# Dense graph attention on one core: three rotating PSUM banks, rows of the next block made early, and every second Relu of head 1 on VectorE

## The chip, the core and the metric

The kernel runs on one core of a Trainium2 chip. A core has TensorE (PE, matmuls into PSUM), VectorE (DVE), ScalarE (ACT), GpSimd (POOL) and SyncE, which each work through a queue of their own, and 16 DMA engines. The metric is the device time of one execution in microseconds; the profile is one execution recorded by the hardware profiler.

## The reference

Four residual layers act on a graph of 3125 nodes with 128 features and 100000 edges, each after a layer norm and a Relu: a mean over neighbours, three layers of graph attention, an aggregation with minimum, maximum and deviation, and a two-layer mean. The change is in the second of them. Its core, cut:

```python
xs = (h @ Ws).reshape(N, H, C)                  # H = 4 heads of C = 32
alpha_s, alpha_d = sum(xs * a_s), sum(xd * a_d)
e = leaky_relu(alpha_s[src] + alpha_d[dst], 0.2)
ex = exp(e - segment_max(e, dst)[dst])
alpha = ex / (segment_sum(ex, dst)[dst] + EPS)
out = segment_sum(xs[src] * alpha[:, :, None], dst) + bias
# three times, with a relu between
```

## The kernel before

Attention is computed densely. A matrix A of edge counts (source by target) was made earlier; for each pair of nodes the weight is the count times the exponential. A layer `g` goes over 8 blocks `J` of 400 targets (`CH`), a block over 25 tiles `n` of 128 sources (`NT`), so a layer has 200 tiles and the stage 600. In a tile each of the four heads passes through a "soft" buffer of 128x400:

- Heads 0 and 1: ScalarE makes a Relu of the block's row plus the source's number (`half_bend`, L879), two tiles ahead; GpSimd adds another row to both heads in one instruction of 128x800 (L719). Together these are the leaky Relu.
- Heads 2 and 3: VectorE makes it in one instruction (`bend`, L1853), from a row that stays in PSUM (`psV`) and one in SBUF.
- ScalarE takes the exponential of each head into PSUM (`exponent`, L891). There are three banks for it: `psE[2]` and `psE[3]` are the same one.
- VectorE caps it and multiplies by the counts, back into the soft buffer (`weigh`, L1861).
- TensorE sums over the sources (L1302) with an operand `xs_1` in which the features of a head stand beside 32 columns of ones: 64 columns give numerator and denominator of a head. Heads 0 and 1 go into `psL`, heads 2 and 3 into `psZ`, each pair as two column tiles.

At a block's end ScalarE copies the denominators (`totals`, L869), VectorE divides (`divide`, L1885 and L1888), ScalarE writes the new features (`layer_rows`, L861). TensorE opens the accumulators of the next block (L1298) when `divide` has read them.

Each block needs rows of its own, made in tiles 16 to 23 of the block before: `levels` is 25 matmuls into `psR` (L1230), VectorE's `highest` takes the top level out of the exponent's bits (L1829, L1830), `top_rows` and `own_rows` are two matmuls with four output rows (L1236, L1240), VectorE's `top` and `near` work on four partitions (L1835, L1841 to L1843), `spread_row` spreads each of four rows over 128 partitions (L1247), ScalarE's `near_row` copies it out (L854, L856), `keep_rows` writes the two rows that stay in PSUM (L1253). The order of the work on each engine is written out by hand in the loops over `t`; between engines stand only semaphores. `summed` counts the tiles that TensorE has summed: the soft buffers have four places for heads 0 and 1 (`A_SLOTS`) and three for heads 2 and 3 (`MOVING`).

Of the kernel before, what the change touches and what calls it, by code (L numbers as in the profile page):

```python
# [5 lines left out]
ALU = mybir.AluOpType  # L6
# [8 lines left out]
H = 4  # L15
# [59 lines left out]
def build(nc, x, src, dst, W0, b0, Ws, Wd, att_s, att_d, gat_b, M_w, M_b, U_w, U_b, gamma, beta,  # L75
# [42 lines left out]
    with ExitStack() as ctx:  # L118
# [31 lines left out]
        LEV = XSW + NT * 6 * C  # L150
        ROWV = LEV + NT * H * LEVELS // 2
        SOFT = MB
        LAST_ROW = SOFT + MOVING * 2 * CH
        BIGW = max(ROOT + NT * D, MB + 2 * DENSE_T * W, LAST_ROW + CH)
        assert ROWV + 9 * CH <= U
# [63 lines left out]
        psE = [quad[:, 512 * i:512 * i + CH] for i in (0, 1, 2, 2)]  # L219
# [66 lines left out]
        for t in range(STEPS):  # L286
# [21 lines left out]
        xs_1 = words(XSW, NT * 6 * C).rearrange("p (t a k) -> p t a k", t=NT, a=2)  # L308
# [6 lines left out]
        row_2 = [words(ROWV, 2 * CH), words(ROWV + 6 * CH, 2 * CH)]  # L315
        row_8 = [[words(ROWV + 4 * CH, CH), words(ROWV + 5 * CH, CH)], [words(ROWV + 8 * CH, CH), words(LAST_ROW, CH)]]
        row_2v = [[words(ROWV + 2 * CH, CH), words(ROWV + 3 * CH, CH)],
                  [apart[:, 3 * NT * H + P // 2 + CH // 2 + h * CH:3 * NT * H + P // 2 + CH // 2 + (h + 1) * CH] for h in range(2)]]
        level = apart[:, 2 * LANE - LEVELS:2 * LANE]
        assert 3 * NT * H + P // 2 + CH // 2 + 2 * CH <= 2 * LANE - LEVELS - 7 * H  # L320
# [3 lines left out]
        bits = lane_x[:].rearrange("p a w -> p (a w)")[:, 0:CH]  # L324
        m_4 = bits[0:H, :]
        v_4 = Z[0:H, 0:CH]
        share = sm[:, 0:CH]
        to_all = lane_s[0:H, :, :]
# [3 lines left out]
        def soft(n, h):  # L332
            if h < 2:
                return pick[:, (2 * (n % A_SLOTS) + h) * CH:(2 * (n % A_SLOTS) + h + 1) * CH]
            return words(SOFT + (2 * (n % MOVING) + h - 2) * CH, CH)

# [102 lines left out]
        sel_rdy = sem("sel_rdy")  # L439
        xs_ps, xs_rdy = sem("xs_ps"), sem("xs_rdy")  # L440
        reach_rdy, reach_ps, diag_rdy = sem("reach_rdy"), sem("reach_ps"), sem("diag_rdy")
# [3 lines left out]
        half_a, bent_p, bent_v, near_ps, soft_rdy = sem("half_a"), sem("bent_p"), sem("bent_v"), sem("near_ps"), sem("soft_rdy")  # L445
# [212 lines left out]
        def _(pool):  # L658
# [55 lines left out]
            for n in range(NT * NH):  # L714
# [3 lines left out]
                pool.wait_ge(half_a, 2 * n + 2)  # L718
# [37 lines left out]
        def _(act):  # L756
# [92 lines left out]

            def near_row(J, h):  # L850

                act.wait_ge(row_ps, H * J + h + 1)
                if h < 2:
                    nc.scalar.mul(row_8[J % 2][h], psR, 1.0 - NEG_SLOPE)  # L854
                to = row_2[J % 2][:, CH * h:CH * h + CH] if h < 2 else row_2v[J % 2][h - 2]
                nc.scalar.mul(to, psR, NEG_SLOPE).then_inc(row_rdy, 1)  # L856

            def layer_rows(g, J):

                act.wait_ge(share_rdy, 4 * (J + 1))  # L860
# [20 lines left out]
            def exponent(n, h):  # L881

                if h == 0:
                    act.wait_ge(bent_p, n + 1)
                elif h >= 2:
                    act.wait_ge(bent_v, 2 * n + h - 1)
                if h < 3 and n:
                    act.wait_ge(weight_rdy, H * n + (-3, -2, 0)[h])
                if h == 3:
                    act.wait_ge(weight_rdy, H * n + 3)  # L890
                nc.scalar.activation(psE[h], soft(n, h), ACT.Exp, bias=s_all[:, 2, n % NT, h:h + 1]).then_inc(soft_rdy, 1)  # L891
# [3 lines left out]
            for g in range(3):  # L895
                for t in range(NT):
# [3 lines left out]
                    for k in range(2):  # L900
                        ins = nc.scalar.copy(xs_1[:, t, :, 2 * C * k:2 * C * k + C],
                                             psY[t % 2][:, 0:D].rearrange("p (a h c) -> p h a c", a=2, h=2)[:, k, :, :])
                    ins.then_inc(xs_rdy, 1)
                act.wait_ge(lev_rdy, 2 * g + 1)
                nc.scalar.activation(lev, lev, ACT.Exp, scale=STEEP * 0.6931471805599453).then_inc(xs_rdy, 1)
                for c in range(NCH):
                    J = NCH * g + c
                    if c == 0:
                        for h in range(H):
                            near_row(J, h)  # L910
                        for n in range(NT * J, NT * J + 2):
                            half_bend(n, 0)
                            half_bend(n, 1)
                    for t in range(NT):
                        n = NT * J + t
                        ahead = c < NCH - 1 or t < NT - 2
# [12 lines left out]
                        if c < NCH - 1 and 19 <= t < 19 + H:  # L929
                            near_row(J + 1, t - 19)  # L930
# [155 lines left out]
        def _(pe):  # L1086
# [134 lines left out]
            def levels(g, J):  # L1221

                for late in range(2):
                    k = 2 * J + late
                    pe.wait_ge(a_part[k % RING], 16 * (k // RING + 2))
                pe.wait_ge(lev_rdy, 2 * g + 2)
                if J:
                    pe.wait_ge(row_rdy, H * J)
                for t in range(NT):
# [857 lines left out]
```

## Time and profile before

| | us |
|---|---|
| median of three runs | 5264.95 (5263.87 to 5265.28) |
| the profiled execution | 5259.3, span 5257.5 |
| busy in the span: TensorE / VectorE / ScalarE / GpSimd | 3943.7 / 3670.2 / 3263.5 / 1873.8 |
| GpSimd's adds of the attention (L719), 600 | 1131.4 |
| exponentials (L891), 2400 | 705.8 + 659.1 |
| weightings (L1861), 2400 | 682.4 + 650.0 |

The profiled execution's time is 1.8 us more than its span, which lies between its first and its last instruction. Busy time counts an engine's own instructions; an engine that is idle may be waiting for another, and the timeline names in brackets for how long and for whom.

### The profile page before, as it was taken

Reading aid. Unit: us, or ns where it says so; the run is one execution under the profiler, and the core shown is the slowest. Engines: PE = TensorE matmul, PEld = TensorE weight load, DVE = VectorE, ACT = ScalarE, POOL = GpSimd, SP = SyncE. Lnnn points to the kernel's source line nnn. Section 1 sums busy time; section 2 is a strip of 40 time slices with the busy share of each in tenths; the row PEclk is TensorE's granted clock in tenths of the full one; section 3 lists DMA queues with packets and bytes.
Section 4 is the critical chain, followed back from the end, with each engine's and each line's share of the span. In section 5 each row is a group of like instructions: output and inputs, shape, how many; then the busy total and the mean of one; then the engine's idle time right before and its main releaser. Section 6 shows DMA issues by size and latency. Waiting matters only on the chain.

```text
span 5257.5 us, 59119 instructions
## 1 busy us (share of the span) xinstructions
PE 3943.7 (75%) x16302; PEld 1689.8 (32%) x16302; DVE 3670.2 (70%) x8162; ACT 3263.5 (62%) x7606; POOL 1873.8 (36%) x1368
## 2 busy tenths in 40 slices
PE   6999796666666666666666666666669999986899
PEld 3444344111111121111112111111137667654444
DVE  8999784777777757777775777777767777774311
ACT  5888404777667756777775777777757667674100
POOL 0000131444333323333332434444437777773000
PEclk9999896676766666666666676766679999997899
DMA  4444642111111101111111111111026776763566
GB/s 154 157 154 155 228 167 72 39 39 58 39 39 39 60 19 40 39 39 60 40 39 39 40 39 39 39 39 58 0 85 231 239 240 232 241 217 105 183 229 224
DMA packets 387474, 552.25 MB, mean 105 GB/s; under 512 B 23781, under 2 KB 358021, under 8 KB 386922
## 3 DMA queue, kind: packets, MB, share of 16 engines
q1 hardware_dynamic: 358114, 494.48, 27.1%
q0 software_dynamic: 23024, 48.93, 3.4%
q10 hardware_dynamic: 6040, 5.35, 0.4%
q8 instruction: 130, 2.13, 0.2%
q14 instruction: 166, 1.36, 0.1%
HBM read 352.81 MB, written 195.86 MB: 104 GB/s over the span
## 4 chain that ended last, share of the span: by engine, by line
DVE 34%; ACT 19%; PE 17%; issue 11%; DMA 6%; POOL 3%; SPq 2%; ACTq 0%; DVEq 0%; POOLq 0%
DVE pick L1861 12%; PE quad L1109 7%; ACT quad L891 7%; DVE big L1861 6%; ACT pick L879 6%; DVE big L1853 6%; DMA src_bc<-pe_src_d 3%; POOL big L736 2%; PE psS L1230 2%; DMA big<-table_d,src_win 2%; DVE big L1982 2%; PE psZ L1302 2%; PE quad L1430 1%; DVE sm L1885 1%; ACT hT L977 1%
## 5 line engine op out<-in xcount | busy, mean ns | idle before, releaser
L719 POOL TENSOR_TENSOR pick<-pick,big 128x800 f32<-128x800 f32 x600 | 1131.4, 1886 | 1913.7 <-ACT pick L879 1913.7
L891 ACT ACTIVATE quad<-big,keep 128x400 f32<-128x400 f32 x1200 | 705.8, 588 | 770.1 <-DVE big L1861 770.1
L1302 PE MATMUL psZ<-big 128*64 128x400 f32 x2400 | 799.3, 758 | 469.6 <-DVE big L1861 468.2
L1302 PE MATMUL psL<-pick,big 128*64 128x400 f32 x2400 | 794.5, 754 | 207.2 <-DVE pick L1861 206.4
L1861 DVE SCALAR_TENSOR_TENSOR pick<-quad,big 128x400 f32<-128x400 f32 x1200 | 650.0, 572 | 303.3 <-ACT quad L891 302.7
L1861 DVE SCALAR_TENSOR_TENSOR big<-quad,big 128x400 f32<-128x400 f32 x1200 | 682.4, 569 | 113.1 <-ACT quad L891 113.1
L736 POOL DMA_INDIRECT big<-table_d,src_win x672 | 645.4, 960 | 279.5 <-issue 189.3
L879 ACT ACTIVATE pick<-big,keep 128x400 f32<-128x400 f32 x1200 | 735.0, 613 | 0.5
L891 ACT ACTIVATE quad<-pick,keep 128x400 f32<-128x400 f32 x1200 | 659.1, 579 | 3.1 <-POOL pick L719 3.1
L1302 PEld LDWEIGHTS psZ<-big 128*64 128x64 f32 x2400 | 161.2, 179 | 1066.9 <-DVE big L1861 1042.2
L1982 DVE SCALAR_TENSOR_TENSOR big<-big,keep_win,quad 128x256 f32<-128x256 f32 x784 | 375.8, 479 | 152.0 <-ACT quad L1010 81.6
L1302 PEld LDWEIGHTS psL<-pick,big 128*64 128x64 f32 x2400 | 161.2, 178 | 778.0 <-DVE pick L1861 712.4
L795 ACT COPY big<-quad 128x512 f32<-128x512 f32 (+1 forms) x21 | 11.3, 540 | 466.2 <-PE quad L1109 466.2
L1109 PE MATMUL quad<-big 128*128 128x512 f32 (+1 forms) x700 | 278.5, 559 | 6.2 <-issue 5.6
L1376 PE MATMUL psH<-big,pick 128*128 128x384 bf16 x700 | 233.6, 335 | 57.8 <-DVE big L1971 49.6
L831 ACT ACTIVATE big<-quad 128x400 bf16<-128x400 f32 x496 | 232.2, 503 | 57.5 <-PE quad L1169 50.4
L1009 ACT COPY quad<-big 128x128 f32<-128x128 f32 x784 | 199.7, 255 | 108.1 <-DMA big<-table_d,src_win 67.4
L708 POOL TENSOR_TENSOR keep<-big 128x512 f32<-128x512 f32 (+1 forms) x7 | 8.1, 1152 | 685.0 <-DMA big<-A_d 605.2
L1376 PE MATMUL psH<-big,hT 128*128 128x384 bf16 x700 | 232.1, 332 | 22.1 <-DVE big L1971 21.5
L1376 PE MATMUL psS<-big,pick 128*128 128x384 bf16 x700 | 233.3, 334 | 0.0
L1376 PE MATMUL psS<-big,hT 128*128 128x384 bf16 x700 | 231.7, 332 | 0.0
L1010 ACT ACTIVATE quad<-big 128x128 f32<-128x128 f32 x784 | 212.9, 272 | 0.0
(361 smaller groups left out, 6474.5 us busy)
## 6 DMA issues: line engine op xcount, KB each, us to landing
big<-A_d SPq DMA_DIRECT2D x17, 6400.0 KB
rows_d<-big SPq DMA_DIRECT2D x112, 896.0 KB
A_d<-big SPq DMA_DIRECT2D x396, 200.0 KB, 1.9
big<-A_d SPq DMA_DIRECT2D x24, 2600.0 KB, 9.9
big<-A_d SPq DMA_DIRECT2D x24, 2400.0 KB, 9.4
big<-A_d SPq DMA_DIRECT2D x32, 1600.0 KB, 11.0
big<-table_d,src_win POOLq DMA_INDIRECT x672
src_bc<-pe_src_d SPq DMA_DIRECT2D x56, 64.0 KB
```

Source lines behind the costliest of these rows:

```text
L719: pool.tensor_tensor(soft_2[n % A_SLOTS], soft_2[n % A_SLOTS], row_2[J % 2], ALU.add).then_inc(bent_p, 1)
L736: pool.indirect_dma_start(out=rows[:, k, 0:p.table_w], out_offset=None, in_=table_d, in_offset=bass.IndirectOffsetOnAxis(ap=src_win[:, s, ...
L831: nc.scalar.activation(hot_q[:, t % HOTS, j, :], psD[(dist0[t] + n) % 4][:, 0:QW], ACT.Relu).then_inc(hot_s, 1)
L879: nc.scalar.activation(soft(n, h), row_8[J % 2][h], ACT.Relu, bias=s_all[:, 1, t, h:h + 1]).then_inc(half_a, 1)
L891: nc.scalar.activation(psE[h], soft(n, h), ACT.Exp, bias=s_all[:, 2, n % NT, h:h + 1]).then_inc(soft_rdy, 1)
L1010: nc.scalar.mul(psA[n % len(psA)][:, D:2 * D], rows[:, k, :], -1.0).then_inc(sq_rdy, 1)
L1109: ins = nc.tensor.matmul(psT[at % 2][:, 0:n * W].rearrange("f (b w) -> f b w", w=W), rows[:, s, :], abuf[(at + 1) % 2][:, 0:n, W * s:W * s ...
L1302: ins = nc.tensor.matmul(acc[a][64 * k:64 * k + 64, 0:CH], xs_1[:, t, a, C * k:C * k + 2 * C], soft(n, 2 * a + k), start=False, stop=(t == ...
L1376: ins = nc.tensor.matmul(psP[i][:, 0:3 * D].rearrange("p (c w) -> p c w", c=3), is_src[q % 2][:, t, i * P:(i + 1) * P], table_s[:, t, :, 0 ...
L1853: v.scalar_tensor_tensor(soft(n, 2 + h), psV[h], s_all[:, 1, t, 2 + h:3 + h], row_2v[J % 2][h], ALU.add, ALU.max).then_inc(bent_v, 1)
L1861: v.scalar_tensor_tensor(soft(n, h).rearrange("p (b w) -> p b w", w=W), psE[h].rearrange("p (b w) -> p b w", w=W), CAP, a, ALU.min, ALU.mu ...
L1982: v.scalar_tensor_tensor(state[:, k, :], prev[k], kw[:, 1, k:k + 1], psA[n % len(psA)][:, 0:2 * D], ALU.min, ALU.max).then_inc(updated, 1)
```

## The change

Of the four parts, one is on VectorE's and ScalarE's tile: the exponentials go through three banks in turn (`psW`), in the order of heads 3, 0, 1, 2, and an exponential waits for the weighting that was three places earlier. VectorE's `bend` of head 2 is made in the tile itself, that of head 3 one tile ahead. The second: for odd tiles the Relu of head 1 is made on VectorE (`half_bend(n)`, one `tensor_scalar`), and GpSimd's add then waits for both makers. The third: numerators and denominators have banks of their own, `acc[0]` (`psL`) and `acc[1]` (`psZ`), in eight matmuls of 32 columns behind the last weighting of a tile; ScalarE copies both banks (`totals`) and VectorE divides in SBUF. The fourth: the rows of the next block are begun in tile 1, `levels` is given out over tiles 3 to 17, the near rows are cut into three bf16 parts (`cut_row`, `middle_part`) that lie in partitions 0, 32 and 64, and are spread by matmuls in bf16. The scale of the rows is changed by the factor 0.2 of the leaky Relu.

```diff
-        psE = [quad[:, 512 * i:512 * i + CH] for i in (0, 1, 2, 2)]
+        psW = [quad[:, 512 * i:512 * i + CH] for i in range(3)]
...
+        BANK_ORDER = (3, 0, 1, 2)
+        EXP_AT = (2, 3, 4, 1)
+        WEIGH_AT = (2, 3, 4, 1)
+
+        def bank(n, h):
+            return psW[(H * n + BANK_ORDER.index(h)) % len(psW)]
+
+        def bank_free(n, h):
+            at = H * n + BANK_ORDER.index(h) - len(psW)
+            return H * (at // H) + WEIGH_AT[BANK_ORDER[at % H]] if at >= 0 else 0
...
-                pool.wait_ge(half_a, 2 * n + 2)
+                pool.wait_ge(half_a, halves(n))
+                if n % 2:
+                    pool.wait_ge(half_v, n // 2 + 1)
...
             def totals(J):
                 act.wait_ge(summed, NT * (J + 1))
-                for h in range(H):
-                    total = (C, 2 * C)[h % 2]
-                    ins = nc.scalar.copy(share[C * h:C * h + C, :], acc[h // 2][total:total + C, 0:CH])
-                ins.then_inc(totals_rdy, 1)
+                if J:
+                    act.wait_ge(share_rdy, J)
+                nc.scalar.copy(share, acc[0][:, 0:CH])
+                nc.scalar.copy(total_b, acc[1][:, 0:CH]).then_inc(totals_rdy, 1)
...
             def exponent(n, h):
-                if h == 0:
-                    act.wait_ge(bent_p, n + 1)
-                elif h >= 2:
-                    act.wait_ge(bent_v, 2 * n + h - 1)
-                if h < 3 and n:
-                    act.wait_ge(weight_rdy, H * n + (-3, -2, 0)[h])
-                if h == 3:
-                    act.wait_ge(weight_rdy, H * n + 3)
-                nc.scalar.activation(psE[h], soft(n, h), ACT.Exp, ...)
+                act.wait_ge((bent_p, bent_p, bent_2, bent_3)[h], n + 1)
+                if bank_free(n, h):
+                    act.wait_ge(weight_rdy, bank_free(n, h))
+                nc.scalar.activation(bank(n, h), soft(n, h), ACT.Exp, ...)
...
                     for t in range(NT):
-                        exponent(n, 0)
-                        exponent(n, 1)
-                        exponent(n, 2)
-                        if ahead:
-                            half_bend(n + 2, 0)
-                        exponent(n, 3)
-                        if ahead:
-                            half_bend(n + 2, 1)
-                        if c and t == 0:
+                        exponent(n, 3)
+                        if left > 2:
+                            half_bend(n + 2, 0)
+                        exponent(n, 0)
+                        if left > 1 and n % 2:
+                            half_bend(n + 1, 1)
+                        exponent(n, 1)
+                        exponent(n, 2)
+                        if c and t == 1:
                             totals(J - 1)
-                        if c and t == 2:
+                        if c and t == 6:
                             layer_rows(g, J - 1)
-                        if c < NCH - 1 and 19 <= t < 19 + H:
-                            near_row(J + 1, t - 19)
+                        if c < NCH - 1:
+                            if t == 3:
+                                own_row(J + 1)
+                            if t == 20:
+                                middle_part(J + 1)
+                            if t == 21 or t == 22:
+                                near_row(J + 1, t - 21)
+                            if t == 23:
+                                near_row(J + 1, 2)
+                                near_row(J + 1, 3)
...
+            def weighted_sums(n):
+                J, t = n // NT, n % NT
+                if t == 0:
+                    if J:
+                        pe.wait_ge(totals_rdy, J)
+                    nc.tensor.matmul(acc[1][:, 0:CH], of_eps[0:1, :], ones_row[0:1, :], start=True, stop=False)
+                pe.wait_ge(weight_rdy, H * n + H)
+                for h in range(H):
+                    nc.tensor.matmul(acc[0][C * h:C * h + C, 0:CH], xs_1[:, t, C * h:C * h + C], soft(n, h), ...)
+                for h in range(H):
+                    ins = nc.tensor.matmul(acc[1][C * h:C * h + C, 0:CH], ones[:, 0:C], soft(n, h), ...)
+                ins.then_inc(summed, 1)
...
                         if c < NCH - 1:
-                            if t == 16:
-                                levels(g, J + 1)
...
+                            if t == 1:
+                                own_rows(g, J + 1)
+                            if 3 <= t < 16:
+                                levels(g, J + 1, t - 3, t - 2)
+                            if t == 16 or t == 17:
+                                levels(g, J + 1, SPLIT + 6 * (t - 16), SPLIT + 6 * (t - 15))
+                            if t == 18:
+                                top_rows(J + 1)
+                            if 20 <= t < 23:
+                                spread_row(J + 1, t - 20)
+                            if t == 23:
+                                spread_row(J + 1, 3)
+                                keep_row(J + 1, 1)
+                                keep_row(J + 1, 0)
...
+            def cut_row(J):
+                high = parts[J % 2][0:H, :]
+                link(v.tensor_copy(high, v_4))
+                link(v.tensor_tensor(m_4, v_4, high, ALU.subtract))
+                link(v.tensor_copy(mid_4, m_4))
+                v.tensor_tensor(parts[J % 2][64:64 + H, :], m_4, mid_4, ALU.subtract).then_inc(near_rdy, 1)
...
+            def half_bend(n):
+                if n >= A_SLOTS:
+                    dve.wait_ge(summed, n - A_SLOTS + 1)
+                v.tensor_scalar(soft(n, 1), row_8[J % 2][1], s_all[:, 1, t, 1:2], 0.0, ALU.add, ALU.max).then_inc(half_v, 1)
...
+            def divide(J):
+                dve.wait_ge(totals_rdy, J + 1)
+                link(v.reciprocal(total_b, total_b))
+                v.tensor_tensor(share, share, total_b, ALU.mult).then_inc(share_rdy, 1)
...
             def tile_weights(n, left):
-                weigh(n, 0)
-                weigh(n, 1)
-                if bends:
-                    bend(n + 1, 0)
-                weigh(n, 2)
-                if bends:
-                    bend(n + 1, 1)
-                weigh(n, 3)
+                weigh(n, 3)
+                bend(n, 0)
+                weigh(n, 0)
+                if left > 1 and n % 2 == 0:
+                    half_bend(n + 1)
+                if left > 1:
+                    bend(n + 1, 1)
+                weigh(n, 1)
+                weigh(n, 2)
...
                         tile_weights(n, NT * (NCH - c) - t)
+                        if c and t == 3:
+                            divide(J - 1)
                         if c < NCH - 1:
-                            if t == 16:
+                            if t == 18:
                                 highest(J + 1)
-                            if t == 17:
-                                top(J + 1)
-                            if t == 18:
+                            if t == 19:
                                 near(J + 1)
-                        if c and t == 0:
-                            divide(J - 1)
+                                cut_row(J + 1)
```

The rows below are the instructions in the order in which each engine gets them, with the semaphores that they wait for. VectorE, one tile in mid-block before (`pick` is a soft buffer of head 0 or 1, `big` one of head 2 or 3):

```order
L1861 SCALAR_TENSOR_TENSOR pick<-quad,big 128x400 [waits soft_rdy] x2
L1853 SCALAR_TENSOR_TENSOR big<-quad,keep,big 128x400 [waits summed]
L1861 SCALAR_TENSOR_TENSOR big<-quad,big 128x400 [waits soft_rdy]
L1853 SCALAR_TENSOR_TENSOR big<-psH,keep,big 128x400 [waits summed]
L1861 SCALAR_TENSOR_TENSOR big<-quad,big 128x400 [waits soft_rdy]
```

VectorE, the same place now, an even tile (the first row is head 2 of the tile before and head 3 of this one):

```order
L1918 SCALAR_TENSOR_TENSOR big<-quad,big 128x400 [waits soft_rdy] x2
L1901 SCALAR_TENSOR_TENSOR big<-quad,keep,big 128x400 [waits summed]
L1918 SCALAR_TENSOR_TENSOR pick<-quad,big 128x400 [waits soft_rdy]
L1911 TENSOR_SCALAR pick<-big,keep 128x400 [waits summed]
L1901 SCALAR_TENSOR_TENSOR big<-psH,keep,big 128x400 [waits summed]
```

The weighting of head 3 has moved to the front, and the Relu (L1911) stands behind the weighting of head 0.

TensorE, the last matmuls of a block and the first of the next, before:

```order
L1302 MATMUL psZ<-big 64x400 [waits weight_rdy]
L1302 MATMUL psZ<-big 64x400
L1298 MATMUL psL<-keep 128x400 [waits share_rdy]
L1302 MATMUL psL<-pick,big 64x400 [waits weight_rdy]
L1302 MATMUL psL<-pick,big 64x400
L1298 MATMUL psZ<-keep 128x400 [waits share_rdy]
```

and now (the tile's last denominators, the opening, and the next tile's sums):

```order
L1303 MATMUL psZ<-big,ones 32x400 x2
L1297 MATMUL psZ<-keep 128x400 [waits totals_rdy]
L1300 MATMUL psL<-pick,big 32x400 [waits weight_rdy]
L1300 MATMUL psL<-pick,big 32x400
L1300 MATMUL psL<-big 32x400 x2
L1303 MATMUL psZ<-pick,ones 32x400 x2
```

One opening is left, it waits for ScalarE's copies instead of VectorE's division, and all sums of a tile stand behind one wait.

ScalarE, tiles 23 and 24 of a block now (L888 copies rows 2 and 3 of the next block):

```order
L918 ACTIVATE quad<-big,keep 128x400 [waits weight_rdy,bent_2]
L888 COPY big<-psS 128x400 [waits row_ps] x2
L918 ACTIVATE quad<-big,keep 128x400 [waits weight_rdy,bent_3]
L911 ACTIVATE pick<-big,keep 128x400 [waits summed]
L918 ACTIVATE quad<-pick,keep 128x400 [waits weight_rdy,bent_p] x2
```

Both copies stand in one tile, ahead of the exponentials of the last one; before, the four rows were copied in four tiles, 19 to 22.

## Rows read from the trace of the kernel before

**Rows 1.** Busy time of each engine in the first attention layer (stretch, length, engines, clock).

```profile
core 0: us, PE busy (x) PEld busy (x) DVE busy (x) ACT busy (x) POOL busy (x), PEclk, DMA share, GB/s
890.00:1844.00 954.00, 639.14 (x1950) 152.43 (x1948) 704.00 (x1282) 684.63 (x1301) 377.09 (x200) 0.69 0.14 43
```

**Rows 2.** Timeline, tiles in mid-block (start, duration, engine, line; idle time in brackets).

```profile
1190.40 1.09 DVE L1861 SCALAR_TENSOR_TENSOR pick<-quad,big 128x400 f32<-128x400 f32 x2 [0.46 <-ACT quad L891]
...
1191.41 0.63 DVE L1853 SCALAR_TENSOR_TENSOR big<-quad,keep,big 128x400 f32<-128x400 f32 x1
...
1191.95 0.56 DVE L1861 SCALAR_TENSOR_TENSOR big<-quad,big 128x400 f32<-128x400 f32 x1
...
1192.43 0.62 DVE L1853 SCALAR_TENSOR_TENSOR big<-psH,keep,big 128x400 f32<-128x400 f32 x1
...
1192.61 0.60 ACT L891 ACTIVATE quad<-big,keep 128x400 f32<-128x400 f32 x1 [0.65 <-DVE big L1861]
...
1193.14 0.61 ACT L879 ACTIVATE pick<-big,keep 128x400 f32<-128x400 f32 x1
...
1193.24 0.57 DVE L1861 SCALAR_TENSOR_TENSOR big<-quad,big 128x400 f32<-128x400 f32 x1 [0.18 <-ACT quad L891]
...
1193.66 1.10 ACT L891 ACTIVATE quad<-pick,keep 128x400 f32<-128x400 f32 x2
...
1193.83 1.89 POOL L719 TENSOR_TENSOR pick<-pick,big 128x800 f32<-128x800 f32 x1 [1.99 <-ACT pick L879]
...
1194.27 1.09 DVE L1861 SCALAR_TENSOR_TENSOR pick<-quad,big 128x400 f32<-128x400 f32 x2 [0.46 <-ACT quad L891]
```

**Rows 3.** Timeline, GpSimd's add of the same tile in two successive blocks.

```profile
1139.05 1.88 POOL L719 TENSOR_TENSOR pick<-pick,big 128x800 f32<-128x800 f32 x1 [8.87 <-ACT pick L879]
...
1258.71 1.89 POOL L719 TENSOR_TENSOR pick<-pick,big 128x800 f32<-128x800 f32 x1 [8.57 <-ACT pick L879]
```

**Rows 4.** Timeline, operations at a change of block.

```profile
1198.57 4.59 PE L1230 MATMUL psS<-big 128*128 128x400 bf16 x25
...
1203.19 0.57 DVE L1829 TENSOR_SCALAR lane_x<-psS 128x400 int32<-128x400 int32 x1 [5.51 <-PE psS L1230]
...
1203.80 0.37 DVE L1830 TENSOR_SCALAR lane_x<-lane_x 128x400 f32<-128x400 int32 x1
...
1210.57 0.68 DVE L1835 TENSOR_SCALAR lane_x<-psS,ends 4x400 f32<-4x400 f32 x1 [3.12 <-PE psS L1236]
...
1217.66 0.56 DVE L1841 TENSOR_TENSOR Z<-lane_x,psS 4x400 f32<-4x400 f32 x1 [3.12 <-PE psS L1240]
...
1218.25 0.35 DVE L1842 TENSOR_SCALAR Z<-Z 4x400 f32<-4x400 f32 x1
...
1249.21 0.98 ACT L869 COPY sm<-psZ 32x400 f32<-32x400 f32 x2
...
1250.22 2.65 DVE L1885 RECIPROCAL sm<-sm 128x400 f32<-128x400 f32 x1 [1.97 <-ACT sm L869]
...
1254.13 0.51 PE L1298 MATMUL psL<-keep 1*128 1x400 bf16 x1 [8.59 <-DVE sm L1888]
```

**Rows 5.** Timeline, VectorE's L1719 beside GpSimd's additions and without them.

```profile
688.21 8.85 POOL L711 TENSOR_TENSOR keep<-keep,big 128x512 f32<-128x512 f32 x6
...
693.15 1.23 DVE L1719 TENSOR_SCALAR has<-deg 128x4 f32<-128x4 f32 x1
...
783.73 0.16 DVE L1719 TENSOR_SCALAR has<-deg 128x4 f32<-128x4 f32 x1
```

**Rows 6.** Timeline, TensorE: one matmul alone, and pairs of column tiles.

```profile
1238.75 0.93 PE L1253 MATMUL quad<-Z,lane_s 4*128 4x400 f32 x2 [0.66 <-DVE big L1853]
...
1240.63 0.89 PE L1302 MATMUL psL<-pick,big 128*64 128x400 f32 x4
...
2028.64 1.60 PE L1302 MATMUL psZ<-big 128*64 128x400 f32 x4 [0.96 <-DVE big L1861]
...
2030.19 1.60 PE L1302 MATMUL psL<-pick,big 128*64 128x400 f32 x4
```

More of the change, by code:

```diff
@@ L847, in _, with own_row, middle_part @@
             normalize(1)
+            def own_row(J):
+                act.wait_ge(lev_ps, 3 * J + 1)
+                nc.scalar.mul(own_4, psR[0:H, :], NEG_SLOPE).then_inc(lead_rdy, 1)
+            def middle_part(J):
+                act.wait_ge(near_rdy, 2 * J + 2)
+                nc.scalar.copy(parts[J % 2][32:32 + H, :], mid_4).then_inc(lead_rdy, 1)
             def near_row(J, h):
@@ L899, in _ @@
                     act.wait_ge(xs_ps, NT * g + t + 1)
[L900 to L903, printed above, removed]
+                    nc.scalar.copy(xs_1[:, t, :], psY[t % 2][:, 0:D]).then_inc(xs_rdy, 1)
                 act.wait_ge(lev_rdy, 2 * g + 1)
@@ L1218, in _, with own_rows @@
             pe.wait_ge(node_out, NT)
[L1221 to L1226, printed above, removed]
+            def own_rows(g, J):
                 if J:
                     pe.wait_ge(row_rdy, H * J)
-                for t in range(NT):
+                nc.tensor.matmul(psR[0:H, :], w_att[:, g, D + H:D + 2 * H], feat[g % 2][:, CH * (J % NCH):CH * (J % NCH + 1)],
+                                 start=True, stop=True).then_inc(lev_ps, 1)
@@ L1230, in levels @@
+            def levels(g, J, first, last):
+                if first == 0:
+                    pe.wait_ge(lead_rdy, 2 * J + 1)
+                for t in range(first, last):
+                    if t == 0 or t == SPLIT:
+                        k = 2 * J + (t == SPLIT)
+                        pe.wait_ge(a_part[k % RING], 16 * (k // RING + 2))
                     ins = nc.tensor.matmul(psR.rearrange("l (b w) -> l b w", w=W), lev[:, t, :, :].rearrange("p h k -> p (h k)"),
                                            marks_of(J, t), start=(t == 0), stop=(t == NT - 1))
-                ins.then_inc(lev_ps, 1)
+                if last == NT:
+                    ins.then_inc(lev_ps, 1)
@@ L1243, in spread_row @@
             def spread_row(J, h):
-                pe.wait_ge(near_rdy, 3 * J + 3)
                 if h:
                     pe.wait_ge(row_rdy, H * J + h)
-                nc.tensor.matmul(psR, to_all[:, h, :], v_4, start=True, stop=True).then_inc(row_ps, 1)
-            def keep_rows(J):
-                for h in range(2):
-                    if J:
-                        pe.wait_ge(bent_v, 2 * NT * J - 1 + h)
-                    nc.tensor.matmul(psV[h], to_all[:, 2 + h, :], v_4, start=True, stop=True).then_inc(near_ps, 1)
@@ L1288, in _ @@
+                        keep_row(J, 0)
                     for t in range(NT):
                         n = NT * J + t
[L1290 to L1303 removed]
@@ L1880, in tile_weights @@
                     dve.sem_inc(ring_used, 1)
-            def divide(J):
-                dve.wait_ge(totals_rdy, J + 1)
-                link(v.reciprocal(share, share))
-                for h in range(H):
-                    own = (0, 3 * C)[h % 2]
-                    v.tensor_tensor(share[C * h:C * h + C, :], acc[h // 2][own:own + C, 0:CH], share[C * h:C * h + C, :],
-                                    ALU.mult).then_inc(share_rdy, 1)
             for g in range(3):
@@ L1896, in _ @@
                         highest(J)
-                        top(J)
                         near(J)
-                        bend(NT * J, 0)
+                        cut_row(J)
                         bend(NT * J, 1)
```

153 lines of the change are left out of this document (74 added, 79 removed).

## The prediction

> **What bounds the kernel now.** I read first the busy times by stage. The three attention layers take more than half of the span, and in the first of them no engine is full: in 954 us VectorE is busy 704, ScalarE 685, TensorE 639 and GpSimd 377 us, for 200 tiles [rows 1]. So this stage is set by waits in a ring, not by one engine's work. The timeline of one tile in mid-block shows the ring [rows 2]. Heads 2 and 3 share a PSUM bank (`psE`), so the exponential of head 3 starts only when VectorE has weighted head 2 (1192.61, 0.65 us idle in front of it, released by L1861). From there: exponential, then Relu (0.53 from start to start), exponential of head 0 (0.52), and 0.61 until VectorE weighs it (1194.27); on VectorE two weightings (1190.40 to 1191.41, 1.01), a bend (0.54), the weighting of head 2 (0.56) and 0.10 until ScalarE starts. These make 3.87, and the weightings of head 0 are indeed 3.87 apart (1190.40, 1194.27). A tile has six ScalarE instructions 0.52 apart (3.1) and on VectorE four weightings (0.48 apart) and two bends (0.54), 3.0: both engines idle some 0.8 us in each tile because of that bank.
>
> The second cost is the change of block. GpSimd's adds of like place in two successive blocks are 119.66 apart [rows 3]; 25 tiles explain 96.8, so 22.8 us go at each change, in the serial passage through level sums, rows and totals. Per layer: 200 tiles x 3.87 = 774, 7 changes x 22.8 = 160, and 20 for the ends, together 954.
>
> **The change, part by part.** *The tile.* Three banks rotate over the heads, so an exponential waits only for the weighting three places earlier: that ring is gone. VectorE gets 300 Relus (every second one of head 1), ScalarE loses them. No row shows such a Relu; the nearest is the two-operation pass over 128x400 in SBUF, 0.37 us (1203.80) [rows 4]; the bounds are 0.28 and 0.63 (a bend). By work alone a tile then costs VectorE 3.02 + 0.19 = 3.2 and ScalarE 5.5 x 0.52 = 2.9.
>
> What sets the tile is, I think, another ring, which the new Relu closes. It stands on VectorE behind the weighting of head 0 of an even tile n, and GpSimd's add for tile n+1 waits for it; the exponential of head 0 of n+1 waits for the add; ScalarE's Relu for n+2 stands behind that exponential; the add for n+2 waits for this Relu, and the weighting of head 0 of n+2, behind it the next VectorE Relu, for that add. Priced from [rows 2, 4]: Relu 0.37, step to GpSimd 0.08 (1193.14 + 0.61 to 1193.83), add 1.89, step to ScalarE 0.10 (the only such step shown is VectorE's, 1191.95 + 0.56 to 1192.61), exponential to the next ScalarE instruction 0.52, Relu 0.61, step 0.08, add 1.89, step 0.10, exponential 0.58, step 0.03, weighting 0.48. Sum 6.73 for two tiles, 3.37 for one. It exceeds the 3.2 of VectorE, so it decides, by little. Now the add is hidden wholly: ScalarE makes both Relus of a tile two tiles ahead, so the add is done long before its exponential. In the new order that cover is gone.
>
> *TensorE.* Per tile it had four sums with 64 output columns in two pairs; it gets eight with 32 columns, four into `psL`, four into `psZ`, all behind the last weighting. Two side by side cost as much as one: four records in 0.89 at the high clock (1240.63), one matmul's two in 0.93 (1238.75), and at the low clock pairs follow each other 1.55 apart [rows 6]. If four also go side by side a tile costs 2 x 1.55 = 3.1 at 1.2 GHz and about 1.7 at 2.4 GHz. Then the sums of tile n must end before ScalarE's first Relu of n+4, about 3.1 us behind the last weighting of n: just enough even at the low clock. The Trainium skill (TensorE: Matmul & The Clock Gate, "Part 3: Packing small matmuls") measures 2.38 times for three column tiles. By that efficiency, as an estimate from the page, four would take 1.26 times one, some 3.9 us a tile at the low clock and 2.0 at the high; no row here shows four.
>
> *The change of block.* Five items, each against the end E of the tile's last weighting, when ScalarE has been free for 0.66 us. (a) The sums of a block's tile 0 now wait until ScalarE has copied both totals at the end of tile 1: 2 x 0.5 (1249.21), 0.06, the opening matmul 0.44 (1254.13), then 3.1, so E + 4.0. ScalarE needs that for a Relu that it reaches at E + 0.9, and the copies themselves cost it 1.0: with 0.2 slack, 4.0. The other inserted work (a row on ScalarE, the level sums, 0.18 each by 1198.57, one per tile from tile 3) lies beside the tiles: 1.0, bounds 0 and 3. (b) The division: 2.65 (1250.22) and one product of 0.57, 3.25; I add 0.95 for the port, below: 4.2. (c) Bits of the top level: 0.61 + 0.28 (1203.19, 1203.80), and half a microsecond until the last six level sums are done: 1.4. (d) Near rows and their cut into three bf16 parts: eight linked passes on four partitions, 0.68, then 0.56 and 0.36 in turn (1210.57, 1217.66, 1218.25), 4.25 with the gaps, and 0.95 for the port: 5.2. (e) Copies of the four rows: the first two hold ScalarE 1.0 each, of which 0.3 is slack, and the first also waits some 0.5. The fourth is queued directly behind the third in tile 23, but its matmul stands behind that tile's sums: ScalarE stops until E + 3.8 (low clock) or E + 2.2, and all exponentials of tile 24 queue behind it; 4.1 between the two. Together 6.0. Sum 21.8, with bounds 16 and 28: hardly less than the 22.8 of now. Many waits were taken out, but three new ones (a, d, e) stand in single queues.
>
> *The port.* The trace shows that a VectorE pass from SBUF to SBUF can be held while GpSimd adds: 128x4 elements took 1.23 us beside an add (693.15) and 0.16 without (783.73) [rows 5]. The Trainium skill (SBUF — State Buffer, "SBUF: two separate sides") calls it an exclusive lock, held for the whole instruction; the trace agrees. For the new Relu it should cost nothing: the weighting ahead of it needs the add of tile n, and the add of n+1 needs the Relu, so no add is in flight. The passes of (b) and (d) can meet one: 0 to 1.89, depending on whether the tile's number is odd, on average 0.95 each.
>
> *The rest.* The passage at the head of a layer trades shorter bf16 spreads for the longer cut; the copies of the features before it hide behind TensorE's matmuls. I take both at nothing, bounds 10 us faster or slower in all.
>
> **Sum.** Per layer 200 x 3.37 = 673, 7 x 21.8 = 153, ends 20: 846 instead of 954, 108 less, 325 for three. The profiled execution took 5259.3 (span 5257.5), so 4934; the runs' median is 5.65 higher: **4940 us**.
>
> **The rivals.**
> - *VectorE bounds and the changes of block are hidden better* (the high clock holds, no port waits): T = 3.2, b = 16 give 772 a layer, 4725. For it: the ring exceeds VectorE's work by only 0.17. Against: rows (d) and (e) are serial whatever the clock. Chance 0.12.
> - *TensorE becomes the bound*: of four column tiles only two run together. Four rounds of 0.78 at the high clock, which such a busy engine would keep, 3.1, with levels and mode changes about 3.6; everything that waits for it at a block's change is later, b = 28: 720 + 196 + 20 = 936, 5210. Against: two tiles show no loss. Chance 0.15, a quarter of it no longer faster. The 2.38 of the Trainium skill's page named above would put TensorE between this case and the forecast.
> - *Slower: the eight sums run one after another.* 8 x 0.78 = 6.2 a tile at the high clock, 200 x 6.2 + 7 x 16 + 20 = 1372 a layer, 6520. It decides from 4.2 us of TensorE a tile on (954 less 7 x 16, by 200). For it: no 32-column matmul is in the trace. Against: pairs do overlap. Chance 0.05.
> - *Slower: each VectorE Relu meets an add after all*, up to 1.89, of which the ring passes on most: 300 x 1.7 = 510, 5450. By the order of the waits it cannot. Chance 0.03.
> - *The new waits eat all the gain*: b = 38 by (a) and (e) at the low clock throughout: 5270. Chance 0.05.
>
> **How the numbers follow.** The forecast itself has 0.60 and its own range of 4800 to 5060 (T 3.3 to 3.45, b 18 to 26). Below it lies the first rival, above it the second. Leaving out the lowest of the one, and the last three rivals with part of the second, the range is 4760 to 5120. A run of this kernel can tell 0.2% (10 us) from no change. Faster: 0.60 + 0.12 + 0.11 of the second rival + 0.01 of the last = 0.84; same 0.03 (0.01 and 0.02 of the same two); slower 0.13, the rest.
>
> **What would show it.** In mid-block GpSimd's adds stand in pairs, 6.7 us for two, each released by VectorE's Relu and ScalarE's in turn; VectorE idles before the weighting of head 0, released by ScalarE, which waits for GpSimd; hardly any wait of head 3 for head 2. The new Relu takes 0.3 to 0.45. Eight matmuls fill 3.1 (low clock) or 1.7. At a block's change: ScalarE idle 3 to 4 us before the Relu in tile 2, and 2 to 4 before the fourth row copy. Wrong it would be if VectorE is full in mid-block (tile at 3.2), if the eight matmuls take over 4 us, if the Relu's mean is over 1 us, or if a change of block costs less than 16 or more than 28.

## The result, and the profile after

The changed kernel takes **4827.6 us** (4824.3 to 4836.7) against 5264.4 of the kernel before: a ratio of 0.917 (95% interval 0.916 to 0.919), 437 us faster where 325 were forecast. The profiled execution has a span of 4828.8 instead of 5257.5, 428.7 less.

The busy times of the first layer, from its first add to its last (columns as in [rows 1], whose stretch was a little wider):

```profile
880.00:1675.00 795.00, 435.89 (x3420) 115.12 (x3420) 715.99 (x1377) 621.96 (x1171) 376.34 (x200) 0.86 0.15 49
```

VectorE is now busy 90% of the layer. In mid-block (the middle tiles of a block of 25) GpSimd's adds follow one another in unequal steps (timeline of GpSimd: start, duration, and in brackets its idle time and who ended it):

```profile
920.73 1.89 POOL L741 TENSOR_TENSOR pick<-pick,big 128x800 f32<-128x800 f32 x1 [1.26 <-ACT pick L911]
924.33 1.88 POOL L741 TENSOR_TENSOR pick<-pick,big 128x800 f32<-128x800 f32 x1 [1.72 <-DVE pick L1911]
927.48 1.89 POOL L741 TENSOR_TENSOR pick<-pick,big 128x800 f32<-128x800 f32 x1 [1.26 <-ACT pick L911]
```

One release by ScalarE's Relu, one by VectorE's, and 6.75 us for the two: 3.375 a tile. The links of that ring, from one VectorE Relu to the next, stand in the timeline of all engines:

```profile
1034.61 0.42 DVE L1911 TENSOR_SCALAR pick<-big,keep 128x400 f32<-128x400 f32 x1
...
1035.17 1.88 POOL L741 TENSOR_TENSOR pick<-pick,big 128x800 f32<-128x800 f32 x1 [1.72 <-DVE pick L1911]
...
1037.09 0.60 ACT L918 ACTIVATE quad<-pick,keep 128x400 f32<-128x400 f32 x1 [0.34 <-POOL pick L741]
1037.62 0.61 ACT L911 ACTIVATE pick<-big,keep 128x400 f32<-128x400 f32 x1
...
1038.31 1.88 POOL L741 TENSOR_TENSOR pick<-pick,big 128x800 f32<-128x800 f32 x1 [1.26 <-ACT pick L911]
...
1040.23 1.12 ACT L918 ACTIVATE quad<-pick,keep 128x400 f32<-128x400 f32 x2
...
1040.86 0.58 DVE L1918 SCALAR_TENSOR_TENSOR pick<-quad,big 128x400 f32<-128x400 f32 x1
...
1041.35 0.42 DVE L1911 TENSOR_SCALAR pick<-big,keep 128x400 f32<-128x400 f32 x1
```

The Relu ends at 1035.03, the add starts 0.14 later; it ends at 1037.05, the exponential of head 0 starts 0.04 later; ScalarE's next Relu ends at 1038.23, and the next add starts 0.08 later. It ends at 1040.19, the next exponential of head 0 starts 0.04 later, VectorE's weighting follows, and behind it the next Relu at 1041.35. From Relu to Relu VectorE is busy 6.58 of 6.75 us, so by its busy share alone it would seem to be the bound; experiment 1 tells the two apart. Among ScalarE's waits in the layers none of an exponential for a weighting is left.

TensorE at its two clocks (two tiles; each matmul leaves two records, which stand in successive rounds, and x2 counts the records of two heads):

```profile
1036.58 0.53 PE L1300 MATMUL psL<-pick,big 128*32 128x400 f32 x2 [1.59 <-DVE big L1918]
1036.60 0.53 PE L1300 MATMUL psL<-big 128*32 128x400 f32 x2
...
1036.94 0.51 PE L1300 MATMUL psL<-pick,big 128*32 128x400 f32 x2
...
1037.62 0.51 PE L1303 MATMUL psZ<-pick,ones 128*32 128x400 f32 x2
...
1059.73 0.88 PE L1300 MATMUL psL<-pick,big 128*32 128x400 f32 x2 [7.29 <-DVE big L1918]
...
1061.73 0.88 PE L1303 MATMUL psZ<-pick,ones 128*32 128x400 f32 x2
```

The granted clock is 1.00 from 1036 to 1039.5 and 0.50 from 1059.5 to 1062. Four rounds start 0.67 apart at the low level (1.2 GHz) and 0.35 at the high one (2.4 GHz), 2.7 and 1.4 us a tile: the records of all four heads start within 0.02 us of each other, so all four column tiles run side by side.

At a change of block, from the timeline of the second block:

```profile
1052.61 2.13 POOL L741 TENSOR_TENSOR pick<-pick,big 128x800 f32<-128x800 f32 x1 [1.26 <-ACT pick L911]
1053.04 1.92 DVE L1888 CAST big<-Z 4x400 bf16<-4x400 f32 x1
...
1061.66 1.89 POOL L741 TENSOR_TENSOR pick<-pick,big 128x800 f32<-128x800 f32 x1 [6.92 <-DVE pick L1911]
...
1074.10 0.49 ACT L888 COPY big<-psS 128x400 f32<-128x400 f32 x1 [3.37 <-PE psS L1283]
```

The cast of a near row takes 1.92 us beside an add (in every second block; 0.36 in the blocks between), and ScalarE stops 3.37 before the copy of the fourth row. The waits of ScalarE between 890 and 3400 us, nearly the whole of the three layers (total, times, longest), show both stops that the prediction placed in ScalarE's queue:

```profile
ACT quad L918 <- DVE big L1901: 284.6, 313, 4.7
ACT quad L918 <- POOL pick L741: 89.9, 261, 1.0
ACT big L888 <- PE psS L1283: 64.5, 37, 4.1
ACT pick L911 <- PE psZ L1303: 61.4, 21, 3.0
```

L888 copies the rows (item e), L911 is the Relu that waits for the sums held back by the totals (item a), 21 times for 21 changes.

**Where the 429 us came from.** From the start of the first add to that of the last the three layers take 794.7, 797.6 and 797.7 (before 928.7, 934.6, 928.7): 402 less. The first add of all starts 10.6 earlier, the two gaps between layers are 6.0 shorter each, the time after the last add 4.0.

### The profile page after: what moved, and what is told of

Read it like the earlier page. It is cut to its first block, busy times and chain, and to the rows that moved or that the text cites. A ratio compares the mean times of both kernels' runs of the same rounds, so it can differ in the third digit from the quotient of the medians.

```text
span 4828.8 us, 69161 instructions
## 1 busy us (share of the span) xinstructions
PE 3370.3 (70%) x20934; PEld 1591.1 (33%) x20934; DVE 3734.0 (77%) x8487; ACT 3100.6 (64%) x7231; POOL 1875.8 (39%) x1368
## 4 chain that ended last, share of the span: by engine, by line
DVE 36%; PE 17%; POOL 11%; ACT 10%; issue 7%; DMA 7%; SPq 2%; POOLq 0%; DVEq 0%; ACTq 0%
DVE pick L1918 9%; POOL pick L741 8%; DVE big L1901 7%; DVE big L1918 7%; PE quad L1143 7%; ACT quad L918 4%; POOL big L758 3%; DMA big<-table_d,src_win 3%; DMA src_bc<-pe_src_d 3%; DVE pick L1911 2%; PE psL L1300 2%; DVE big L2035 2%; PE psZ L1303 2%; PE quad L1475 1%; DVE lane_x L1924 1%
## 5 line engine op out<-in xcount | busy, mean ns | idle before, releaser
L1300 PE MATMUL psL<-pick,big 128*32 128x400 f32 x2400 | 629.8, 609 | 946.7 <-DVE big L1918 945.8
L1918 DVE SCALAR_TENSOR_TENSOR pick<-quad,big 128x400 f32<-128x400 f32 x1200 | 682.7, 569 | 100.9 <-ACT quad L918 100.6
L1300 PE MATMUL psL<-big 128*32 128x400 f32 x2400 | 629.9, 609 | 0.0
L1303 PE MATMUL psZ<-pick,ones 128*32 128x400 f32 x2400 | 609.4, 592 | 0.0
L1303 PE MATMUL psZ<-big,ones 128*32 128x400 f32 x2400 | 609.3, 591 | 0.0
L911 ACT ACTIVATE pick<-big,keep 128x400 f32<-128x400 f32 x900 | 552.7, 615 | 61.9 <-PE psZ L1303 61.4
L1300 PEld LDWEIGHTS psL<-pick,big 128*32 128x32 f32 x2400 | 97.7, 118 | 1218.1 <-DVE big L1918 1191.7
L1901 DVE SCALAR_TENSOR_TENSOR big<-psH,keep,big 128x400 f32<-128x400 f32 x600 | 375.5, 626 | 17.3 <-ACT big L888 17.3
L1901 DVE SCALAR_TENSOR_TENSOR big<-quad,keep,big 128x400 f32<-128x400 f32 x600 | 374.2, 624 | 0.0
L1303 PEld LDWEIGHTS psZ<-pick,ones 128*32 128x32 f32 x2400 | 161.3, 128 | 332.2 <-issue 332.2
```

The costliest lines, as they stand in the source:

```text
L911: nc.scalar.activation(soft(n, h), row_8[J % 2][h], ACT.Relu, bias=s_all[:, 1, t, h:h + 1]).then_inc(half_a, 1)
L1300: nc.tensor.matmul(acc[0][C * h:C * h + C, 0:CH], xs_1[:, t, C * h:C * h + C], soft(n, h), start=(t == 0), stop=(t == NT - 1))
L1303: ins = nc.tensor.matmul(acc[1][C * h:C * h + C, 0:CH], ones[:, 0:C], soft(n, h), start=False, stop=(t == NT - 1))
L1901: v.scalar_tensor_tensor(soft(n, 2 + h), psV[h], s_all[:, 1, t, 2 + h:3 + h], row_2v[J % 2][h], ALU.add, ALU.max).then_inc((bent_2, bent_3 ...
L1918: v.scalar_tensor_tensor(soft(n, h).rearrange("p (b w) -> p b w", w=W), bank(n, h).rearrange("p (b w) -> p b w", w=W), CAP, a, ALU.min, AL ...
```

## Experiments

All are edits of the changed kernel; times are medians, compared with its 4827.6. Beside the experiments the kernel before took 5258.6 to 5264.4, so a few us between two kernels tell nothing. "Layers" is the sum of the three stretches from first to last add, 2390.0 there.

**1. The Relus back on ScalarE.**

```diff
-                        if left > 1 and n % 2:
-                            half_bend(n + 1, 1)
+                        if left > 2:
+                            half_bend(n + 2, 1)
...
-                if left > 1 and n % 2 == 0:
-                    half_bend(n + 1)
```

(with the counts that GpSimd waits for, and the first Relus of a layer)

> All Relus of head 1 go back to ScalarE, both Relus of a tile made two tiles ahead; the rest as in the change. Ring theory (the add's release by VectorE's late Relu sets 3.375 us a tile): that ring is gone, a tile costs ScalarE's six instructions, 3.12 to 3.2, so 600 x 0.2 = 120 us faster than the change: 4710 (4660 to 4770); GpSimd's adds stand evenly, none released by VectorE. Rival (balance: the new kernel gains because ScalarE was relieved): ScalarE at 3.2 plus its waits is the bound, 3.45 to 3.6 a tile, 4870 to 4960.

4740.2 us, ratio to before 0.901 (0.899 to 0.902); layers 2291.3. The adds stand evenly:

```profile
1030.66 1.88 POOL L739 TENSOR_TENSOR pick<-pick,big 128x800 f32<-128x800 f32 x1 [1.23 <-ACT pick L909]
1033.77 1.88 POOL L739 TENSOR_TENSOR pick<-pick,big 128x800 f32<-128x800 f32 x1 [1.24 <-ACT pick L909]
```

3.11 apart, against 3.375. The Relu takes 0.33 us of VectorE's time (1034.61 to 1034.94, where the `bend` behind it starts), 0.17 a tile; a VectorE that was simply full would have given back that much, and the tile gave back 0.26. So the part of the change that moves Relus to VectorE costs 87 us: the gain comes from the other parts, and the ring through VectorE's Relu limits them. The balance theory falls. Now ScalarE sets the tile: from 1114 to 1135 it is busy for all of the 21.00 us. With it full, a change of block costs more, 20.5 instead of 17.9 us, which takes 55 of the 155 us that 600 tiles gave. The edit alters two things, the engine of the Relu and how far ahead it is made (two tiles instead of one); all Relus on ScalarE one tile ahead were not tried.

**2. VectorE's Relu one tile earlier.**

```diff
-                if left > 1 and n % 2 == 0:
-                    half_bend(n + 1)
+                if left > 2 and n % 2:
+                    half_bend(n + 2)
```

(with the first such Relu ahead of each layer's tiles)

> VectorE keeps its 300 Relus but makes each two tiles ahead of its tile instead of one. Ring theory: the ring opens, a tile costs VectorE's work, 3.2, 600 x 0.17 = 100 us faster than the change: 4725 (4690 to 4780), Relu still 0.42. Lock theory (the Relu may stand only where no add is in flight): the Relu now meets GpSimd adds, its mean goes to 0.9 to 1.6, VectorE's tile to 3.45 to 3.8, 4870 to 5080.

4984.5 us, ratio 0.947 (0.946 to 0.948), 157 slower than the change. The lock theory held. Groups of VectorE and GpSimd, and one of the Relus beside its add:

```profile
L1911 DVE TENSOR_SCALAR pick<-big,keep 128x400 f32<-128x400 f32 x300 | 370.6, 1235 | 0.0
...
1246.82 1.87 POOL L741 TENSOR_TENSOR pick<-pick,big 128x800 f32<-128x800 f32 x1 [2.52 <-ACT pick L911]
1246.90 2.01 DVE L1911 TENSOR_SCALAR pick<-big,keep 128x400 f32<-128x400 f32 x1
```

In the change the same 300 Relus take 125.5 us, 418 ns each. The hold adds 245 us of VectorE's time; less the 100 that the open ring was expected to be worth, 145 slower would follow, as an estimate; 157 were measured. In this place the Relu is early and meets the adds; other early places were not tried.

**3. Heads 2 and 3 share a bank again, heads 0 and 1 have their own.**

```diff
-            return psW[(H * n + BANK_ORDER.index(h)) % len(psW)]
+            return psW[min(h, 2)]
```

(with the waits for a free bank that belong to it)

> The rotation is undone alone: heads 0 and 1 have a bank each and heads 2 and 3 share one, as before the change; the rest as in the change. Theory (the shared bank made the old ring): the ring from the weighting of head 2 to the exponential of head 3 is back, with the new Relu in it every second tile, 3.9 to 4.1 us a tile, 600 x 0.5 to 0.7 = 315 to 430 us slower than the change: 5140 to 5260. Rival (the gain comes from the new sums, the Relu and the passage, not from the banks): a tile stays at 3.4 to 3.5, 4830 to 4900.

5116.5 us, ratio 0.972 (0.970 to 0.973), 289 slower, a little less than the range expected. ScalarE's largest wait is again the exponential of head 3 for the weighting of head 2 (L1917; the row is of 890 to 3400 us, and the third layer ends at 3692):

```profile
ACT quad L917 <- DVE big L1917: 506.1, 459, 1.8
```

In the change that wait does not occur. Eight tiles from the middle of a block cost 4.04 each (median of the 24 blocks; the change has 3.39 by that measure). Without the rotation two thirds of the gain are gone.

**4. The fourth row's spread ahead of the sums of tile 23.**

```diff
+                        if c < NCH - 1 and t == 23:
+                            spread_row(J + 1, 3)
                         weighted_sums(n)
...
                             if t == 23:
-                                spread_row(J + 1, 3)
```

> The spread of the fourth row stands on TensorE ahead of the sums of tile 23 instead of behind them. Theory of item (e): ScalarE's stop of 3.3 us before the fourth copy shrinks to 0.7, a block's change costs 1.3 to 2.6 us less, 21 changes: 27 to 55 us faster than the change, 4785 (4770 to 4805). Rival (the time is lost anyway to the next wait, that for the totals in tile 1): within 10 us of 4828.

4794.6 us, ratio 0.911 (0.910 to 0.912), 33 faster; layers 2351.6. Of the same waits:

```profile
ACT pick L911 <- PE psZ L1303: 61.6, 21, 3.0
...
ACT big L888 <- PE psS L1283: 18.5, 35, 0.7
```

The stop for the fourth row is down to 18.5 us in all, the other is untouched. ScalarE waits 46 us less, and the layers are 38 shorter.

**5. The totals copied at the end of tile 0** (`if c and t == 0:` instead of `t == 1`).

> ScalarE copies the totals of the block before at the end of tile 0 instead of tile 1. Theory of item (a): the sums of tile 0 are no longer late by the copies, ScalarE's 3 us before the Relu of tile 2 go, 21 x 2 to 3 = 42 to 63 us faster than the change, 4775 (4760 to 4800). Rival (the copies then wait for the last sums of the block before, so the stop only moves): within 15 us of 4828, or up to 20 us slower.

4791.7 us, ratio 0.910 (0.908 to 0.911), 36 faster, short of the 42 expected; layers 2343.5, 46 less. The Relu's wait of 61.4 is gone; the copies themselves (L901) now wait a little for the last sums of the block before:

```profile
ACT big L888 <- PE psS L1283: 67.8, 30, 4.2
...
ACT sm L901 <- PE psZ L1303: 17.8, 21, 2.3
```

**6. Both moves.**

> The two moves together: the fourth row's spread ahead of the sums of tile 23, the totals at the end of tile 0. Theory (items (a) and (e) are stops in different tiles, each paid by itself): the gains add, 33 + 36 us, 4759 (4750 to 4770). Rival (they share one delay, so that the second finds little left): 35 to 45 us, 4785 to 4793.

4732.0 us, ratio 0.900 (0.899 to 0.901): 96 faster, more than the sum of 69; layers 2292.6, 97 less against 38 and 46. That lies outside the ranges of both theories. The moves do not share a delay; together they gain somewhat more than apart, and why was not settled. The waits of rows and totals on ScalarE fell together from 64.5 + 61.4 + 4.6 to 22.7 + 0 + 7.6, 100 us.

**7. Both moves, and all Relus on ScalarE.**

> All Relus on ScalarE, and the two moves. Theory (the tile costs ScalarE's 3.18 and the stops at a block's change go besides): 4740 - 69 = 4671 (4655 to 4690). Rival (ScalarE, now full, has no slack in which the copies of rows and totals could lie, so the moves bring half): 4705 (4690 to 4740).

**4636.4 us**, ratio 0.882 (0.880 to 0.883): 191 faster than the change, and below the theory's range. The theory took the moves at 69 us together; beside experiment 1 they gave 104, near the 96 of experiment 6. In mid-block ScalarE is full (21.00 of 21 us, 1104 to 1125), but over 400 us with changes of block in them it is busy 356, VectorE 376: the slack lies at the changes, and there the moves still paid. This is the best of the kernels run.

**8. The division behind an odd tile.**

```diff
-                        if c and t == 3:
+                        if c and n % 2 and t in (3, 4):
                             divide(J - 1)
```

> The division of a block's sums stands behind tile 3 or 4, whichever has an odd number in the whole count, instead of always behind tile 3. Theory of the port (behind an even tile GpSimd's add for the tile after next starts while VectorE is in the division and holds its product, 1.49 instead of 0.57 us; behind an odd tile no add can start): the product takes 0.57 in all blocks, 11 blocks x 0.9 = 10 us faster than the change, 4818 (4810 to 4828). Rival (the longer product is hidden in the ring or has another cause): products of 1.49 remain, within 5 us of 4828.

4831.8 us, ratio 0.919 (0.917 to 0.920): no gain. The product's three durations (shortest, median, longest in ns), first in the change, then here:

```profile
L1925 DVE TENSOR_TENSOR sm<-sm,lane_x x24: 574/1030/1487, 994.2 to 3411.2; 128x400 f32<-128x400 f32 x24
```

```profile
L1925 DVE TENSOR_TENSOR sm<-sm,lane_x x24: 574/574/575, 1006.1 to 3419.3; 128x400 f32<-128x400 f32 x24
```

Half the theory: the hold comes by the tile's parity, as said, and goes with it; but the time did not follow. The adds around a division with a held product in the change, then the same adds here, and ScalarE's wait for the fourth row here (64.5, 37, 4.1 in the change):

```profile
993.41 1.87 POOL L741 TENSOR_TENSOR pick<-pick,big 128x800 f32<-128x800 f32 x1 [1.26 <-ACT pick L911]
1000.71 1.89 POOL L741 TENSOR_TENSOR pick<-pick,big 128x800 f32<-128x800 f32 x1 [5.42 <-DVE pick L1911]
```

```profile
1001.98 1.89 POOL L741 TENSOR_TENSOR pick<-pick,big 128x800 f32<-128x800 f32 x1 [1.26 <-ACT pick L911]
1008.67 1.89 POOL L741 TENSOR_TENSOR pick<-pick,big 128x800 f32<-128x800 f32 x1 [4.80 <-DVE pick L1911]
...
ACT big L888 <- PE psS L1283: 71.7, 34, 4.4
```

So the hold does cost 0.6 us where it stands (7.30 against 6.69 between the adds), but the stop for the fourth row grew by 7.2 us in all, about as much as the division gave, and the layers are 2389.0 against 2390.0. Why that stop grew was not settled.

**9. The two sums of one head next to each other** (one loop over the heads instead of two, so that neighbours in the queue share 32 columns).

> The eight sums of a tile in another order: the two sums of one head, which share 32 columns, one behind the other, instead of four heads and then four heads. Theory (matmuls go side by side only with those of other columns that stand next to them in the queue): only pairs overlap, ten passes of 0.665 instead of four at the low clock, 4.5 to 5.3 us a tile at 1.2 GHz and 2.3 to 2.7 at 2.4 GHz; 4950 (4850 to 5150), clock higher than 0.885. Rival (each column group has its own order): 2.66 a tile as now, within 15 us of 4828.

4836.2 us, ratio 0.919 (0.917 to 0.920): within the 15 us of the rival. The four column groups advance each in its own order (granted clock 1.00): the denominators of head 0 stand second in the queue, but they start at 1057.31, behind the numerators of all four heads:

```profile
1056.61 0.54 PE L1300 MATMUL psL<-pick,big 128*32 128x400 f32 x2 [2.03 <-DVE big L1917]
1056.64 0.54 PE L1300 MATMUL psL<-big 128*32 128x400 f32 x2
...
1057.31 0.51 PE L1302 MATMUL psZ<-pick,ones 128*32 128x400 f32 x2
...
1057.64 0.51 PE L1302 MATMUL psZ<-pick,ones 128*32 128x400 f32 x2
```

**10. The features copied in two halves again at the layers' heads.**

> ScalarE copies the features of each tile at a layer's head in two halves of 64 columns, as before the change, instead of one of 128. Theory (the single copy shortened the heads by 27 us in all): 25 copies more of about 0.33 in each head, 8 us a head where ScalarE sets the pace, 3 to 8 where TensorE does: 4840 (4835 to 4850), and the gaps between the layers' adds 70 to 72. Rival (the heads are shorter because TensorE runs them at the higher clock): within 5 us of 4828, gaps at 66.

4832.4 us, ratio 0.918 (0.917 to 0.919), and the gaps are 65.4 and 65.0, not 70. So the single copy did not shorten the heads. Nor did the clock, as the rival had it: in the gap between the layers a tile's features take 0.85 us before and after alike. Rows show where the time is: at the end of the first layer, before,

```profile
1826.93 0.98 ACT L869 COPY sm<-psL 32x400 f32<-32x400 f32 x2 [1.60 <-PE psZ L1302]
...
1834.03 0.63 ACT L861 ACTIVATE big<-sm,gat_bT 128x400 f32<-128x400 f32 x1 [5.13 <-DVE sm L1888]
```

and after:

```profile
1680.39 0.49 ACT L901 COPY sm<-psL 128x400 f32<-128x400 f32 x1 [2.28 <-PE psZ L1303]
...
1684.61 0.63 ACT L893 ACTIVATE big<-sm,gat_bT 128x400 f32<-128x400 f32 x1 [3.33 <-DVE sm L1925]
```

From the first copy of totals to the row's bias 7.1 us became 4.2, and from the last add to that copy 7.7 became 5.8: 4.8 of the 6.0. This is read, not tried.

## Why the prediction was right, and where its sizes were off

- **The shared bank made the old ring (right).** Experiment 3 brings it back, with 289 us.
- **The new ring sets the tile (right).** Forecast 6.73 for two tiles, measured 6.75, link by link; experiment 1 opens it, with 0.26 us a tile. It exceeds VectorE's own work by little, as forecast: VectorE idles 0.17 in those 6.75. The Relu took 0.42 (0.37 assumed), its step to GpSimd 0.14 (0.08), the step to ScalarE 0.04 (0.10).
- **The Relu in the ring meets no add (right).** 418 ns in the mean, and 1235 in the other place tried. The slower rival "each VectorE Relu meets an add" has thus a true mechanism, for another order. The Trainium skill's page "SBUF — State Buffer" ("SBUF: two separate sides") describes such a lock for a whole instruction; experiment 2 agrees, 2.01 us beside an add of 1.87.
- **TensorE hides in mid-block (right, and better).** 2.7 and 1.4 us a tile against 3.1 and 1.7. The Trainium skill's 2.38 for three column tiles ("TensorE: Matmul & The Clock Gate", Part 3) would have meant 3.9 and 2.0 by the estimate made; these runs show no such loss.
- **The block change (mechanism right, size off).** It was put at 21.8. A layer's first to last add is 796.7 in the mean; less 199 x 3.375 that is 125, or 17.9 for each of seven changes. Over 21 changes 3.9 less make 82 us, of which the tile's 3.375 for 3.37 takes back 3. Item by item, in the change of 1046 to 1101: bits of the top level 0.8 (1.4 assumed), near rows and cut 5.5 with the port (5.2), row copies 5.3 (6.0), totals 3.8 with nothing for level sums and rows (5.0), division 3.1 (4.2), together 18.5. So no single item failed: TensorE's sums end 0.4 sooner than assumed (2.7 us at the low level), and the other inserted work, put at 1.0, cost 0.2 here and some 0.7 in every second block. Experiments 4 and 5 gave back 1.8 and 2.2 a change (38 and 46 by 21); ScalarE's waits for row and totals fell by 46 and some 50, so nearly all of what these stops cost ScalarE was on the path. The port's 0.95 on the division was too much: the hold occurs in every second block, as the parity said, and costs 0.6 there, and experiment 8 shows that the kernel is no faster without it.
- **Heads and ends (wrong: "nothing, 10 us at most").** They gave 27. Four copies of totals and four products became two and one; the prediction counted that inside the layers, and forgot that at a layer's end nothing covers it. The 10.6 of the first add of all are not explained: it starts between 877 and 888 in these runs, whatever was edited, at 884 in the mean, and at 890 before. So a good part of them is scatter between executions, which happened to point the same way.
- **Two slips in the sums of the rivals.** By their own terms the first rival comes to 4719, not 4725, and the last to 5280, not 5270. Neither bears on the forecast.

Together 82 - 3 + 27 = 106, for the 104 between the 429 of the profiled spans and the 325 forecast. Nearly all these errors point one way, and the gain is a third larger than forecast; the time lies near the lower end of the forecast's own range of 4800 to 5060, and a change of block, at 17.9, just below its 18 to 26.

## What to carry to other kernels

When a bank or buffer is freed, look for the ring that closes next, and add it up over as many tiles as its order repeats in: here a Relu that another engine made one tile ahead closed a ring of two tiles through three engines, and all Relus on ScalarE, two tiles ahead, were 87 us faster. A stop in a single queue (a copy that waits for a matmul that stands behind a tile's sums) is best removed by the order of issue: two moved lines gave 96 us. Removed work counts where nothing covers it: at the ends of the layers 4.8 of 6.0 us could be read off it, though this was not tried.

## What the runs showed of the hardware

- Four column tiles of 32 columns (128 rows, fp32, 400 elements) run side by side with no loss seen: the first two rounds of four take 0.87 us at the high level (1036.58 to 1037.45), one matmul alone 0.93 [rows 6]. Each column group keeps its own order: with another queue order among groups the kernel took 4836.2 instead of 4827.6 us.
- A `tensor_scalar` or a cast of VectorE from SBUF to SBUF that starts beside a GpSimd add was held until the add ended: 2.01 instead of 0.42 us (128x400), 1.92 instead of 0.36 (4x400). The reciprocal (128x400, SBUF to SBUF) was not: 2.64 or 2.65 in all 24 blocks, beside adds too (991.55 to 994.19, with adds running from 990.27 to 992.15 and from 993.41), and it did not hold them.
